# Two edge sums of a graph network: the last chunk of every ring turn comes row by row from SyncE

## The chip, the cores and the metric

The program runs on one core of a Trainium2 chip. The metric is the device time of one execution in microseconds; before the change its median over three runs is 3943.59 us (3941.09 to 3946.39).

## The reference, cut to what matters

```python
# x: 6250 nodes x 256, src/dst/edge_weight: 100000 edges
x = x + gnn0(layernorm(x))      # h = x @ W; agg[row] += edge_weight * h[col]; batch norm; relu
x = x + ffn0(layernorm(x))      # top-k tokens through a gelu MLP
x = x + gnn1(layernorm(x))      # aggr[row] += edge_weight * x[col]; two-layer MLP; row norm
x = x + moe(layernorm(x))       # 8 experts, top 2
```

Both graph layers hold the same sum over edges: for each edge, one row of 1 KB (256 float32) is read by its column number, weighted, and added to the node of its row number. These two sums are what the change touches.

## The kernel before, in words

The kernel first sorts the edges by tile of 128 nodes (the first block, up to about 377 us in the trace), and packs them into 784 chunks (`CHUNKS`) of 128 edges. A chunk that straddles two node tiles is used twice, so there are 832 slots (`SLOTS`), worked off in 52 steps of 16 (`STEPS`, `GB`), four at a time (`GSEM`).

`aggregate` is one such sum and is called twice: with `table[0]` (the first sum, about 385 to 1375 us) and with `through_mlp` set (the second sum, about 1786 to 2798 us). In it:

- GpSimd (POOL) issues one indirect DMA for each chunk (L1081). It brings the chunk's 128 rows of 1 KB from the table in HBM into one of `RING` = 56 places of the tile `got`. Before every pair of chunks it waits on `pairs_summed`, the count of pairs of slots that TensorE has finished, so that a place is free again.
- TensorE (PE) waits for the landing of four chunks at a time (`gathered`), reads the four places of its slots from `slot_ring` into registers (L1167), and multiplies each chunk with a 128x128 routing matrix (L1174). A slot is one product, recorded as two matmuls.
- VectorE (DVE) builds the routing matrices (L1090) and adds each product to the accumulator A of its node tile (L1107).
- Beside it, each finished node tile goes through a small chain on TensorE, ScalarE (ACT) and VectorE: one product and statistics in the first sum (`NodeRows`), a two-layer MLP, two norms and router scores in the second (`GraphTiles`).
- SyncE (SP) is nearly idle. In the first sum it loads and keeps some parameters (until L1060) and then waits. In the second sum it stores each normalised tile to `expert_table`: `store_normal` (L960) waits for the tile, issues one DMA of 128 KB, waits until it has landed (L963) and only then counts `stored` up, on which `normalise` of the next tile waits. There is one buffer `normal`. To find the tile's number SP reads two registers per step from SBUF (L1039, L1041).

The order of the slots and their places in the ring are worked out by VectorE at the end of the first block, in `order_slots` (L515 to L520), and turned by TensorE and stored from there; the block ends when those tables are back in SBUF and the last scatter of edge records has landed.

Of the kernel before, what the change touches and what calls it, by code (L numbers as in the profile page):

```python
# [5 lines left out]
ALU = mybir.AluOpType  # L6
# [8 lines left out]
P = 128  # L15
# [25 lines left out]
RING = 56  # L41
SLOT_COLUMNS = -(-SLOTS // P)
# [13 lines left out]
assert EP * EJ == E and NG * GC == EJ and RUNS_D * RUN * P < BIG and CHUNKS % GSEM == 0 and SLOTS % GB == 0 and RING % GSEM == 0 and NT % GROUP == 0 and GROUPS % 2 == 1  # L56
# [6 lines left out]
class Steps:  # L63
# [28 lines left out]
def build(nc, x, src, dst, edge_weight, g0_w, g0_bias, g0_gamma, g0_beta, f0_wr_in, f0_br, f0_w1, f0_b1_in, f0_w2, f0_b2_in,  # L92
# [14 lines left out]
    with ctx:  # L107
# [103 lines left out]
        with ExitStack() as scope, nc.Block() as block:  # L211
# [164 lines left out]
            def _(dve):  # L376
# [114 lines left out]
                def order_slots():  # L491
# [12 lines left out]
                    for f in range(3):  # L504
# [11 lines left out]
                    s(dve.tensor_tensor(past_ring, chunk_of_slot[:].unsqueeze(2).to_broadcast([P, SLOT_COLUMNS, rings]),  # L516
                                        ring_start[:].unsqueeze(1).to_broadcast([P, SLOT_COLUMNS, rings]), ALU.is_ge))
# [314 lines left out]
        class GraphTiles:  # L832
# [5 lines left out]
            def __init__(self, here):  # L838
                self.tile = FinishedTile(here, "g1_")
                self.wr = here("wr", [P, KD, NE])  # L840
                self.normal, self.normal_t = here("normal", [P, D]), here("normal_t", [P, D])
# [4 lines left out]
                self.normal_ready, self.landed, self.stored = sem("g1_normal"), sem("g1_normal_landed"), sem("g1_normal_stored")  # L846
# [100 lines left out]
            def normalise(self, dve, k, t):  # L947
# [5 lines left out]
                wait(dve, self.stored, k)  # L953
                wait(dve, self.normal_turned, k)
                dve.tensor_scalar(self.normal[:], row(X, t), self.ln_moments[:, 0:1], self.ln_inverse[:, 0:1],
                                  ALU.subtract, ALU.mult).then_inc(self.normal_ready, 1)

            def store_normal(self, sp, k, t):
                sp.wait_ge(self.normal_ready, k + 1)
                sp.dma_start(expert_table[:, 0:D].rearrange("(t p) d -> p t d", p=P)[:, bass.ds(t, 1), :],  # L960
                             self.normal[:].rearrange("p (a d) -> p a d", a=1)).then_inc(self.landed, 16)
                sp.wait_ge(self.landed, 16 * k + 16)
                sp.sem_inc(self.stored, 1)  # L963

            def turn_normal(self, pe, k):
                pe.wait_ge(self.normal_ready, k + 1)
                wait(pe, self.normal_out, k)
                for i in range(KD):
                    ins = pe.transpose(psum[:, self.BANK_OF, i * P:(i + 1) * P], self.normal[:, i * P:(i + 1) * P], ident[:])
# [32 lines left out]

        def aggregate(rows, name, through_mlp, source, local, weight):
# [5 lines left out]
            FINISHES = STEPS - 1  # L1009
            with ExitStack() as scope, nc.Block() as block:  # L1010
                here = lambda what, shape, dt=F32: sb(name + what, shape, dt, scope)
                got = here("got", [P, RING, D])
# [14 lines left out]
                def gathered_after(q):  # L1027

                    earlier = -(-(CHUNKS // GSEM - q % 8) // 8) if through_mlp else 0
                    return (earlier + q // 8 + 1) * (16 * GSEM)  # L1030
# [18 lines left out]
                def _(sp):  # L1049
# [3 lines left out]
                    if not through_mlp:  # L1053
# [6 lines left out]
                        sp.dma_start(f0_first[:].rearrange("p (k n) -> p k n", k=KD), f0_w1.rearrange("(k p) n -> p k n", p=P)).then_inc(params, 16)  # L1060
                        sp.wait_ge(params, 144)
                    if through_mlp:
                        for k in range(FINISHES):
# [1134 lines left out]
```

## Time and profile before

| | |
|---|---|
| median of 3 runs | 3943.59 us (3941.09 to 3946.39) |
| span of the profiled execution | 3521.7 us |
| time of the profiled execution beside its span | not stated; median less span is 421.9 us |
| POOL, indirect DMAs of both sums (L1081) | 1568 x 952 ns |
| first sum, 405 to 1385 us: PE / DVE / ACT / POOL busy | 618 / 611 / 61 / 731 us of 980 |
| second sum, 1787 to 2770 us: PE / DVE / ACT / POOL busy | 702 / 725 / 135 / 745 us of 983 |

The span runs from the first to the last instruction that the profiler recorded. A group's line gives busy time and mean duration, then the idle time of the engine in front of it and what ended that idle time. "issue" is time in which the engine waited for nothing that the profile shows. SPq, ACTq, DVEq and POOLq are the sequencers of the engines: register work and the issuing of DMAs, which don't count as busy.

### The profile page before, as it was taken

How to read it: one execution, taken by the hardware profiler on the slowest of the kernel's cores; microseconds unless marked ns; L12 is line 12 of the kernel's file. 1: busy time of each engine (PE TensorE's matmuls, PEld its weight loads, DVE VectorE, ACT ScalarE, POOL GpSimd, SP SyncE). 2: the span in 40 equal slices, each digit the busy share in tenths (PEclk: the TensorE clock that was granted, in tenths of full speed). 3: DMA queues.
4: the chain of work that ended last, by engine and by line, in shares of the span. 5: the costliest groups of instructions: out<-in, count | busy, mean ns of one | idle time of the engine just before them, and what ended most of it. 6: DMA issues, size and time to landing. Idle time of an engine off the chain costs nothing. (4 is left out here: it accounts for less than half of the span.)

```text
span 3521.7 us, 55765 instructions
## 1 busy us (share of the span) xinstructions
PE 2647.4 (75%) x15311; PEld 2239.6 (64%) x15311; DVE 2613.3 (74%) x6603; ACT 1008.4 (29%) x2073; POOL 2208.3 (63%) x2147
## 2 busy tenths in 40 slices
PE   6888466666666665899967677777776569999998
PEld 4777344454444444789945555555555459999997
DVE  6999566666666666969967777777777778888886
ACT  0011000000000002545511111111111168888886
POOL 0455577777777774345557777777777326666664
PEclk9999687878878787899978888888788779999999
DMA  3011433333333332000133333333333447776775
GB/s 98 10 44 33 120 105 105 105 105 105 105 105 105 105 105 73 1 2 31 37 103 111 113 112 111 113 113 111 113 111 113 133 134 216 213 218 211 219 211 140
DMA packets 164679, 389.01 MB, mean 110 GB/s; under 512 B 46378, under 2 KB 95602, under 8 KB 151019
## 3 DMA queue, kind: packets, MB, share of 16 engines
q0 software_dynamic: 99072, 233.49, 24.4%
q1 hardware_dynamic: 65387, 152.94, 12.8%
q8 instruction: 96, 1.57, 0.2%
q14 instruction: 124, 1.02, 0.1%
HBM read 343.97 MB, written 42.98 MB: 110 GB/s over the span
## 5 line engine op out<-in xcount | busy, mean ns | idle before, releaser
L1081 POOL DMA_INDIRECT g_got<-table,e_source x1568 | 1492.1, 952 | 506.5 <-issue 458.9
L1174 PE MATMUL psum<-g_got,g_route 128*128 x3328 | 1087.2, 485 | 642.0 <-DMA g_got<-table,e_source 253.6
L1174 PEld LDWEIGHTS psum<-g_got,g_route 128*128 128x128 f32 x3328 | 760.9, 239 | 888.4 <-issue 763.5
L1107 DVE TENSOR_TENSOR A<-A,psum 128x256 f32 x1664 | 698.5, 420 | 523.6 <-PE psum L1174 345.1
L1090 DVE TENSOR_SCALAR g_route<-columns,e_local,e_weight 128x128 f32<-128x128 f32 x1664 | 472.5, 363 | 17.7 <-issue 12.9
L368 POOL DMA_INDIRECT records<-rec,place x120 | 148.7, 1239 | 220.6 <-ACT rec L580 122.0
L1582 POOL TENSOR_TENSOR f_ht_lo<-f_ht,f_ht_hi 128x512 fp32r<-128x512 f32 x100 | 133.7, 1341 | 187.8 <-ACT f_ht_hi L1531 182.1
L142 PE MATMUL psum<-e_xt_hi,e_w_hi 128*128 128x256 f32 x832 | 238.0, 286 | 5.5 <-issue 5.3
L142 PE MATMUL psum<-e_w_hi,e_ht_hi 128*128 128x256 f32 x832 | 233.1, 280 | 3.1 <-DVE e_w_lo L1981 3.1
L144 PE MATMUL psum<-e_xt_hi,e_w_lo 128*128 128x256 f32 x832 | 233.8, 281 | 0.0
L143 PE MATMUL psum<-e_xt_lo,e_w_hi 128*128 128x256 f32 x832 | 233.7, 281 | 0.0
L143 PE MATMUL psum<-e_w_lo,e_ht_hi 128*128 128x256 f32 x832 | 233.0, 280 | 0.0
L144 PE MATMUL psum<-e_w_hi,e_ht_lo 128*128 128x256 f32 x832 | 232.8, 280 | 0.0
L1860 POOL DMA_INDIRECT out<-e_y,e_homes x104 | 179.1, 1722 | 63.4 <-POOL e_homes L1856 47.6
L661 PE MATMUL psum<-to_row,value 125*48 125x128 f32 x1600 | 191.1, 281 | 31.5 <-DVE to_row L554 30.8
L661 PEld LDWEIGHTS psum<-to_row,value 125*48 125x48 f32 x1600 | 180.5, 127 | 52.0 <-issue 38.1
L2126 ACT ACTIVATE e_ht<-psum,e_b 128x256 f32<-128x256 f32 x416 | 181.8, 473 | 100.0 <-PE psum L144 100.0
L830 ACT COPY A<-psum 128x256 f32 x52 | 19.4, 372 | 575.3 <-DVE node_stats L818 575.3
L1987 DVE TENSOR_TENSOR e_ht_lo<-e_ht,e_ht_hi 128x512 fp32r<-128x512 f32 x208 | 138.6, 689 | 50.9 <-ACT e_ht_hi L2130 49.4
L1973 DVE TENSOR_TENSOR e_w_lo<-e_w,e_w_hi 128x2048 fp32r<-128x2048 f32 x52 | 119.2, 2293 | 58.4 <-ACT e_w_hi L2135 58.4
L142 PEld LDWEIGHTS psum<-e_xt_hi,e_w_hi 128*128 128x128 f32 x832 | 157.6, 189 | 5.9 <-issue 5.9
L142 PEld LDWEIGHTS psum<-e_w_hi,e_ht_hi 128*128 128x128 f32 x832 | 158.9, 191 | 3.3 <-issue 3.3
(420 smaller groups left out, 5198.5 us busy)
## 6 DMA issues: line engine op xcount, KB each, us to landing
e_w<-in_m_w SPq DMA_DIRECT2D x104, 1024.0 KB, 5.0
g_got<-table,e_source POOLq DMA_INDIRECT x1568, 2.8
expert_table<-g_normal SPq DMA_DIRECT2D x52, 128.0 KB
table<-xn SPq DMA_DIRECT2D x49, 128.0 KB, 1.7
X<-in_x SPq DMA_DIRECT2D x1, 6144.0 KB
table<-f_ring SPq DMA_DIRECT2D x24, 256.0 KB, 2.1
out<-X SPq DMA_DIRECT2D x1, 6144.0 KB
f_w<-in_f_w SPq DMA_DIRECT2D x2, 1024.0 KB, 7.3
```

The lines of the kernel that those rows point to most:

```text
L142: pe.matmul(to, a_hi, b_hi, start=first, stop=False)
L143: pe.matmul(to, a_hi, b_lo, start=False, stop=False)
L144: return pe.matmul(to, a_lo, b_hi, start=False, stop=last)
L368: pool.indirect_dma_start(by_row, bass.IndirectOffsetOnAxis(ap=place[:, g, d:d + 1].bitcast(U32), axis=0), rec[:, g % 2, d, :, :].rearrang ...
L661: ins = pe.matmul(sums_of(u), value[0:EP, u, j, :, :].rearrange("p f c -> p (f c)"), to_row[0:EP, u, j, :], start=j == 0, stop=j == GC - 1)
L1081: pool.indirect_dma_start(got[:, c % RING, :], None, rows, bass.IndirectOffsetOnAxis(ap=source[:, c:c + 1].bitcast(U32), axis=0)).then_inc ...
L1090: ins = dve.tensor_scalar(route[:, (n * GB + j) % (GB + GSEM), :], columns[:], local[:, n * GB + j:n * GB + j + 1], weight[:, n * GB + j:n ...
L1107: dve.tensor_tensor(to, to, sums_of(c), ALU.add).then_inc(added, 1)
L1174: ins = pe.matmul(sums_of(c), route[:, c % (GB + GSEM), :], row(got, at[j % GSEM]), start=True, stop=True)
L1860: pool.indirect_dma_start(out, bass.IndirectOffsetOnAxis(ap=homes[:, u, j:j + 1].bitcast(U32), axis=0), y[:, u, j, :], None, bounds_check= ...
L1987: dve.tensor_tensor(ht_lo[:, u, of], ht[:, of], ht_hi[:, u, of], ALU.subtract).then_inc(h_split, 1)
L2126: act.activation(ht[:, b * MT:(b + 1) * MT], psum[:, 1 + b % 4, 0:MT], ACT.Gelu, bias=b1[:, one, b]).then_inc(hid_out, 1)
```

## The change

In every turn of the ring but the first, the last chunk (numbers 111, 167, ..., 783: 13 chunks of each sum) isn't brought by POOL's indirect DMA. SyncE brings its 128 rows one by one: it loads the row numbers of half a chunk (64 words) from HBM into one partition, reads eight of them into registers with one statement, and issues eight DMAs of one row (1 KB) each with the register as source address (`HandRows.fetch`). These chunks rotate over three places at the end of `got` (`HAND_PLACES`), which grows from 56 to 58 places, so that SyncE may begin up to three turns ahead; it waits on `pairs_summed` for a place. TensorE waits for such a chunk on a semaphore of its own place.

`order_slots` works out the new places with six more VectorE operations. In the second sum, SyncE no longer stores the normalised tiles: ScalarE issues these stores, from two alternating buffers with a semaphore each, and waits for the last two at the end. `normalise` then waits for the store and the transpose of the tile before the last one.

```diff
+HAND = RING - 1
+HAND_PLACES = 3
+PLACES = HAND + HAND_PLACES
+ROUND = HAND_PLACES * RING
...
+def place_of(c):
+    return HAND + c // RING % HAND_PLACES if c % RING == HAND else c % RING
...
-                    rings = CHUNKS // RING
-                    past_ring = passed_of[:, :, 0:rings]
-                    s(dve.tensor_scalar(ring_start[:], columns[:, 1:1 + rings], float(RING), None, ALU.mult))
-                    s(dve.tensor_tensor(past_ring, chunk_of_slot[:]..., ring_start[:]..., ALU.is_ge))
-                    s(dve.tensor_reduce(ring_no, past_ring, AX.X, ALU.add))
+                    def count_started(to, every):
+                        n = (CHUNKS - 1) // every
+                        ...   # the same three operations, n columns wide
+                    count_started(turn_no, RING)
+                    count_started(hand_no, ROUND)
                     s(dve.tensor_scalar(slot_tile_f, slot_values[:, 1, :], rank_tile_f[:, 0:1], None, ALU.add))
-                    dve.scalar_tensor_tensor(ring_no, ring_no, -float(RING), chunk_of_slot[:], ALU.mult, ALU.add).then_inc(map_ready, 1)
+                    s(dve.scalar_tensor_tensor(hand_no, hand_no, -float(HAND_PLACES), turn_no, ALU.mult, ALU.add))
+                    s(dve.scalar_tensor_tensor(ring_no, turn_no, -float(RING), chunk_of_slot[:], ALU.mult, ALU.add))
+                    s(dve.scalar_tensor_tensor(hand_no, ring_no, float(HAND), hand_no, ALU.is_equal, ALU.mult))
+                    dve.tensor_tensor(ring_no, ring_no, hand_no, ALU.add).then_inc(map_ready, 1)
...
-                wait(dve, self.stored, k)
-                wait(dve, self.normal_turned, k)
+                wait(dve, self.stored[k % 2], 16 * (k // 2))
+                wait(dve, self.normal_turned, k - 1)
...
-            def store_normal(self, sp, k, t):
-                sp.wait_ge(self.normal_ready, k + 1)
-                sp.dma_start(expert_table[...], self.normal[:]...).then_inc(self.landed, 16)
-                sp.wait_ge(self.landed, 16 * k + 16)
-                sp.sem_inc(self.stored, 1)
+            def store_normal(self, act, k, t):
+                act.wait_ge(self.normal_ready, k + 1)
+                act.dma_start(expert_table[...], self.normal[:, k % 2:k % 2 + 1, :]).then_inc(self.stored[k % 2], 16)
...
+        class HandRows:
+            LOAD = 8
+            HALF = P // 2
...
+            def ask(self, sp, i, h):
+                c = self.chunks[i]
+                sp.dma_start(self.numbers[:, h, :], kept_fields[0][h * self.HALF:(h + 1) * self.HALF, c:c + 1].rearrange("p a -> a p"),
+                             allow_slow_non_contiguous=True).then_inc(hand_numbers_in, 16)
+
+            def fetch(self, sp, got, rows, pairs_summed, start, end):
+                for r in range(start, min(end, P * len(self.chunks)), self.LOAD):
+                    i, p = divmod(r, P)
+                    h, c = p // self.HALF, self.chunks[i]
+                    if r == 0:
+                        self.ask(sp, 0, 0)
+                    if p == 0 and c >= ROUND:
+                        sp.wait_ge(pairs_summed, (c - ROUND + NT - 1) // 2 + 1)
+                    if p % self.HALF == 0:
+                        sp.wait_ge(hand_numbers_in, 16 * (2 * (self.before + i) + h + 1))
+                    _, nodes = nc.values_load_multi_w_load_instructions(self.numbers[0:1, h, p % self.HALF:p % self.HALF + self.LOAD], ...)
+                    for j in range(self.LOAD):
+                        sp.dma_start(got[p + j:p + j + 1, place_of(c), :], rows[bass.ds(nodes[j], 1), :]).then_inc(hand_landed[(self.before + i) % HAND_PLACES], 16)
+                    if p % self.HALF == 0 and i + h < len(self.chunks):
+                        self.ask(sp, i + h, 1 - h)
...
                             for c in range(first, first + GSEM // 2):
+                                if c in hand.chunks:
+                                    continue
                                 pool.indirect_dma_start(
-                                    got[:, c % RING, :], None, rows,
+                                    got[:, place_of(c), :], None, rows,
...
                             if n >= 3:
                                 tiles_of.keep_normal_turned(act, n - 3)
+                                tiles_of.store_normal(act, n - 3, tile_to_finish(n - 2, mybir.EngineType.Activation))
...
                         tiles_of.keep_result(act, FINISHES)
+                        tiles_of.store_normal(act, FINISHES - 1, tile_to_finish(FINISHES, mybir.EngineType.Activation))
                         tiles_of.keep_normal_turned(act, FINISHES - 1)
```

SyncE's part of both sums is now `hand.fetch(sp, got, rows, pairs_summed, 0, P * CHUNKS)`: in the first sum behind its parameter loads, in the second behind the loads of `GraphTiles`.

## Rows read from the trace of the kernel before

**Rows 1.** The core's span and clock, and POOL's gathers on the page.
```profile
core 0: 3521.7 us, clock 0.868
...
L1081 POOL DMA_INDIRECT g_got<-table,e_source x1568 | 1492.1, 952 | 506.5 <-issue 458.9
```

**Rows 2.** Busy time by stretch: us, PE, PEld, DVE, ACT, POOL, PEclk, DMA share, GB/s.
```profile
405.00:1385.00 980.00, 618.41 (x2163) 468.75 (x2162) 611.05 (x1756) 61.06 (x157) 730.53 (x769) 0.80 0.36 105
1787.00:2770.00 983.00, 701.73 (x2741) 537.79 (x2742) 725.49 (x2286) 134.92 (x447) 744.70 (x783) 0.83 0.39 112
```

**Rows 3.** Timeline of POOL: first and last gather of the first sum, both of the second.
```profile
385.31 0.97 POOL L1081 DMA_INDIRECT g_got<-table,e_source  x1 [9.32 <-DVE e_source L753]
...
1368.60 0.95 POOL L1081 DMA_INDIRECT g_got<-table,e_source  x1 [0.30 <-issue]
...
1786.23 1.02 POOL L1081 DMA_INDIRECT g_got<-table,e_source  x1 [19.94 <-POOLq L1261]
...
2770.30 0.95 POOL L1081 DMA_INDIRECT g_got<-table,e_source  x1 [0.30 <-issue]
```

**Rows 4.** Waits: PE in either sum, POOL in the second (total, times, longest us).
```profile
PE psum L1174 <- DMA g_got<-table,e_source: 143.5, 56, 5.8
...
PE psum L1174 <- DMA g_got<-table,e_source: 110.1, 59, 16.1
...
POOL g_got L1081 <- PE psum L1174: 10.4, 34, 0.3
```

**Rows 5.** Landing of the gathers, 1787 to 2760 us.
```profile
DMA to landing us min/median/max: 2.6/2.8/3.9
```

**Rows 6.** Timeline of SyncE's issued DMAs: start us, us, line.
```profile
362.75 0.25 SPq L335 DMA_DIRECT2D tile_of_rank_row<-rank_tile_i  x1
...
365.16 0.76 SPq L340 DMA_DIRECT2D step_rank<-slot_map  x1
...
367.00 0.36 SPq L342 DMA_DIRECT2D tile_of_rank<-tile_of_rank_row  x1
...
403.21 0.43 SPq L1058 DMA_DIRECT2D f_br_row<-in_f_br  x1
...
404.19 0.29 SPq L1059 DMA_DIRECT2D f_b<-in_f_b_in  x1
404.53 0.38 SPq L1060 DMA_DIRECT2D f_w<-in_f_w  x1
...
1786.94 0.29 SPq L865 DMA_DIRECT2D g_b<-in_g_b  x1
...
1788.48 0.47 SPq L868 DMA_DIRECT2D router_bias<-in_m_br  x1
```

**Rows 7.** SyncE's store of a normalised tile, by instruction (ns min/median/max).
```profile
L960 SPq FUSED_REGOPS  x52: 37/37/42, 1866.5 to 2795.2; - x52
L960 SPq MOVE expert_table<-g_normal x52: 29/29/43, 1866.6 to 2795.3; - x52
L960 SPq DMA_DIRECT2D expert_table<-g_normal x52: 332/332/366, 1866.7 to 2795.3; - x52
```

**Rows 8.** Register loads: one value on SP, one and four values on DVE.
```profile
L1041 SPq TENSOR_LOAD <-tile_of_rank x51: 267/273/292, 1789.6 to 2785.5; - x51
...
L1039 DVEq TENSOR_LOAD <-finish_tile x102: 305/318/333, 440.8 to 2782.8; - x102
...
L1096 DVEq TENSOR_LOAD <-slot_tile x416: 337/344/611, 414.3 to 2773.7; - x139
```

**Rows 9.** Timeline of DVE in `order_slots`.
```profile
358.54 0.26 DVE L516 TENSOR_TENSOR over<-chunk_of_slot,ring_start 128x98 f32<-128x98 f32 x1
...
359.39 0.17 DVE L520 SCALAR_TENSOR_TENSOR slot_columns<-slot_columns,chunk_of_slot 128x7 f32<-128x7 f32 x1
```

**Rows 10.** Timeline of ACT at the end of the second sum.
```profile
2791.87 0.27 ACT L988 ACTIVATE row_numbers<-psum,g_ln_scale 128x8 f32 x1 [1.28 <-PE psum L981]
2792.04 0.19 ACT L903 ACTIVATE g_root<-g_root 128x1 f32<-128x1 f32 x1
```

More of the change, by code:

```diff
@@ L1001, in build, with __init__, wait_landed @@
         gathered = [sem(f"gathered{u}") for u in range(8)]
+        class HandRows:
+            LOAD = 8
+            HALF = P // 2
+            def __init__(self, turns, before):
+                self.chunks = [RING * k + HAND for k in turns]
+                self.before = before
+                self.numbers = expert[:].rearrange("a (h p) -> a h p", h=2)
+            def ask(self, sp, i, h):
[12 more added lines that the diff above has]
+                        sp.wait_ge(hand_numbers_in, 16 * (2 * (self.before + i) + h + 1))
+                    _, nodes = nc.values_load_multi_w_load_instructions(
+                        self.numbers[0:1, h, p % self.HALF:p % self.HALF + self.LOAD], engines=(mybir.EngineType.SP,), min_val=0, max_val=NT * P - 1,
+                        skip_runtime_bounds_check_because="a source is a node")
+                    for j in range(self.LOAD):
+                        sp.dma_start(got[p + j:p + j + 1, place_of(c), :], rows[bass.ds(nodes[j], 1), :]).then_inc(hand_landed[(self.before + i) % HAND_PLACES], 16)
+                    if p % self.HALF == 0 and i + h < len(self.chunks):
+                        self.ask(sp, i + h, 1 - h)
+            def wait_landed(self, pe, q):
+                for i, c in enumerate(self.chunks):
+                    if c // GSEM == q:
+                        pe.wait_ge(hand_landed[(self.before + i) % HAND_PLACES], 16 * P * ((self.before + i) // HAND_PLACES + 1))
@@ L1003, in aggregate, with gathers_of @@
+        hand_numbers_in, hand_landed = sem("hand_numbers_in"), [sem(f"hand_landed{u}") for u in range(HAND_PLACES)]
+        turns = range(1, CHUNKS // RING)
+        hands = (HandRows(turns, 0), HandRows(turns, len(turns)))
+        def gathers_of(q, hand):
+            return [c for c in range(q * GSEM, (q + 1) * GSEM) if c not in hand.chunks]
         def aggregate(rows, name, through_mlp, source, local, weight):
@@ L1009, in aggregate @@
             FINISHES = STEPS - 1
+            hand = hands[through_mlp]
             with ExitStack() as scope, nc.Block() as block:
                 here = lambda what, shape, dt=F32: sb(name + what, shape, dt, scope)
-                got = here("got", [P, RING, D])
+                got = here("got", [P, PLACES, D])
                 route = here("route", [P, GB + GSEM, P])
@@ L1027, in gathered_after @@
                 def gathered_after(q):
-                    earlier = -(-(CHUNKS // GSEM - q % 8) // 8) if through_mlp else 0
-                    return (earlier + q // 8 + 1) * (16 * GSEM)
+                    own = sum(len(gathers_of(at, hand)) for at in range(q % 8, q + 1, 8))
+                    before = sum(len(gathers_of(at, hands[0])) for at in range(q % 8, CHUNKS // GSEM, 8)) if through_mlp else 0
+                    return 16 * (before + own)
                 def sums_of(c):
@@ L1060, in _ @@
                         sp.dma_start(f0_first[:].rearrange("p (k n) -> p k n", k=KD), f0_w1.rearrange("(k p) n -> p k n", p=P)).then_inc(params, 16)
+                        hand.fetch(sp, got, rows, pairs_summed, 0, P * CHUNKS)
                         sp.wait_ge(params, 144)
                     if through_mlp:
-                        for k in range(FINISHES):
-                            tiles_of.store_normal(sp, k, tile_to_finish(k + 1, mybir.EngineType.SP))
-                        tiles_of.store_normal(sp, FINISHES, last_tile(sp))
+                        hand.fetch(sp, got, rows, pairs_summed, 0, P * CHUNKS)
                 @block.gpsimd
@@ L1790, in build @@
             added = [sem("e_added0"), sem("e_added1")]
-            finished = sem("e_finished")
             QUARTER = HB * MT // 4
```

31 lines of the change are left out of this document (21 added, 10 removed).

## The prediction

> **What bounds the kernel now.** I read the span first, then the page's costliest groups, the busy time by stretch, POOL's timeline, the waits, and last SyncE's issued DMAs. The span is 3521.7 us against a median of 3943.6 us; the page gives no time of its own for the profiled execution. I take the 421.9 us between them as lying around the span and unchanged, so that a microsecond saved in the span is one saved in the time [rows 1].
>
> In both sums no engine is full by its busy time: POOL leads with 731 of 980 us and 745 of 983 us, DVE and PE have 611 to 725 [rows 2]. But POOL's gathers are a clock. The first sum's 784 start between 385.31 and 1368.60 us, the second's between 1786.23 and 2770.30 us. That is 983.29 / 783 = 1.2558 us and 984.07 / 783 = 1.2568 us each: 0.95 us of work and 0.30 us of "issue", in which POOL waits for nobody [rows 3]. Its waits for TensorE in the second sum are 34 of at most 0.3 us, as long as that same gap, so they cost nothing; TensorE on its side waits 143.5 us and 110.1 us in all for landings of gathers [rows 4]. So the sums last as long as 784 gathers take, plus the landing of the last one (2.8 us) and the end of the last tiles [rows 5].
>
> **Part 1: 13 gathers fewer per sum.** A hand chunk is skipped in POOL's loop, and nothing takes its place there. 13 x 1.256 = 16.3 us per sum, 32.7 us for both. The last chunk, 783, is a hand chunk itself; it must only be there early enough. For the saving to arrive, TensorE and VectorE must take 56 chunks in 55 x 1.256 = 69.1 us instead of 70.3 us. The landing waits of 143.5 and 110.1 us are the reserve, of which 16.3 us each would be used [rows 4]. This part is all of the gain.
>
> **Part 2: what SyncE needs for it.** A row is a register operation, a move and a DMA, as in the store of a tile by a register: 37 and 29 ns, and the DMA [rows 7]. Between SyncE's instructions lie 0.04 to 0.05 us (404.19 + 0.29 to 404.53) [rows 6]. The trace has the same shape of DMA twice, one row of 1 KB into one partition, issued right behind another DMA: 0.29 us both times (b2, L1059 and L865) [rows 6]. So one row costs 0.037 + 0.029 + 0.29 + 3 x 0.04 = 0.474 us, and 128 rows 60.7 us. Eight numbers are read with one load: on DVE four values cost 344 ns and one 318 ns, so 9 ns for each further one, and on SP 273 + 7 x 9 = 334 ns, with its gap 0.374 us; 16 of them are 6.0 us [rows 8]. The two loads of row numbers gather 64 single words each; the nearest is the one with 52 (0.76 us), so 1.6 us [rows 6]. With 0.1 us for waits a turn costs SyncE **68.4 us**, against the 69.1 us that POOL leaves it.
>
> It need not even be below. In the first sum SyncE is free at 404.9 us [rows 6] and, after the first row numbers (0.8 + 2.8 us), begins its first chunk at 408.5 us; chunk 111 would be due from POOL's beat at 385.3 + 110 x 1.256 = 523.4 us. Less one turn that is 45.9 us ahead (landings on both sides cancel). In the second sum it begins at 1788.95 + 3.6 = 1792.6 us, 62.7 us ahead by the same sum [rows 3, 6]. Over 13 chunks nothing is late as long as a turn stays under 69.1 + 45.9 / 13 = 72.6 us and 73.9 us. The places of the ring allow SyncE to be more than a hundred chunks ahead, so its wait on `pairs_summed` is not what limits it.
>
> The bounds for the row's DMA are 0.25 us (one row stored after a DMA, L335) and 0.36 us (one short row loaded behind two other one-partition loads, L342); the widest row that it could be like is 0.43 us, a DMA over 128 partitions right behind another (L1058) [rows 6]. A turn is then 63.3, 77.4 or 86.3 us. I take 0.29 us, since those two are the same copy. The saving is eaten up where 26 turns are late by 30.2 us in all beyond both reserves of 108.6 us: at 5.3 us per turn over 69.1, so at 0.335 us for the DMA. The margin is 0.05 us per row, which is small. Reading eight numbers in two loads instead of one would cost 5.7 us per turn, and use it up as well.
>
> The Trainium skill speaks against the row here: "DMA: Bandwidth & Descriptors", in the table of instruction costs for descriptors made in hardware under the section on why a DMA increments its semaphore by 16, puts one copy at 512 sequencer cycles for generations before the newest, which at the 1.2 GHz that the page "Trainium Kernel Development and Optimization" (NeuronCore Architecture) states for SyncE is 0.427 us. The trace has both: 0.43 us for 128 partitions in a series, and 0.29 us for one row. By the page's figure the sum would be that of the second rival below.
>
> **Part 3: the stores move to ScalarE.** It issues 52 of them, each a register operation, a move and a DMA of 0.33 us, 0.5 us with gaps, and reads two registers first, 0.7 us with its register operation [rows 7, 8]: 1.2 us per step of 19 us, on an engine that is busy 135 us of 983 [rows 2]. The wait in it, for the normalised tile, stands behind the copy of the same tile's transpose and so is over; what is queued behind it is the next tile's staging copy, and for that TensorE's transpose. In the steady part that is hidden. At the end it isn't: the store of the last tile but one stands before the copy, the scores and the root of the last tile, and the root follows the scores without a gap [rows 10]. I charge **+1.2 us**, between 0 and 3 us (three stores in the tail). SyncE's wait for each landing goes, and with it DVE's for a free buffer; DVE's wait shows nowhere, so I count no gain.
>
> **Part 4: the map.** Three narrow counting operations and three more of 7 columns, 0.17 to 0.26 us with 0.04 us between [rows 9]: 6 x 0.22 = **+1.3 us** in front of the tables that the first block's end waits for. Below, these tables leave later and get out of the way of the last scatters, which could give that back and some more; I keep 0 to +1.3 us, and -4 us for a lucky order.
>
> **Sum.** -32.7 + 1.2 + 1.3 = -30.2 us: 3943.6 - 30.2 = **3913 us**.
>
> **The rivals.**
>
> *SyncE becomes the bound.* If the row's DMA costs 0.36 us instead of 0.29, a turn lasts 77.4 us, 8.3 us more than POOL's. The first sum is then late by 13 x 8.3 - 45.9 = 62 us and the second by 108 - 62.7 = 45 us; less 30.2 us that is +78 us, 4021 us. It decides from 0.335 us on. For it: the row from L342, and that no row of the trace shows many such DMAs in a series, nor eight values read by SP. Against: the two equal copies, both behind another DMA.
>
> *A flat price per DMA.* If each costs 0.43 us whatever its size, a turn is 86.3 us, and the same sum gives 13 x 17.2 x 2 - 108.6 - 30.2 = +308 us, 4252 us. Only this would agree with the page named above; the two rows at 0.29 us and the one at 0.25 us speak against it.
>
> *TensorE and VectorE take over.* If the pair can't go faster than now, the 13 gathers are hidden and only the 2.5 us remain: 3946 us. For it: in the second sum DVE is busy 74% and PE waits often for DVE. Against: 110 us of waits for landings in that sum, 143 us in the first.
>
> *Rows late by a little.* Between 0.32 and 0.335 us for the DMA a part of the gain is lost, 3920 to 3943 us; it is inside the range.
>
> **How the numbers follow.** I give 0.62 to the forecast (its own range 3905 to 3925 us: the low end with the lucky order of part 4, the high end with a turn of about 74 us or twice the tail), 0.08 to rows late by a little, 0.07 to the pair as the bound, 0.18 to SyncE as the bound and 0.05 to the flat price. A measurement here can't tell less than 0.2% (7.9 us) from no change. Faster by more has the forecast and half of the late rows, 0.66. Within 0.2% lie the other half and most of the pair, 0.10. Slower is the rest, 0.24. The range goes from 3905 to 3985 us: it takes in the forecast, the partial cases, the pair, and the lower part of SyncE as the bound, and leaves out about 2 in 10.
>
> **What the profile after would show.** Right: 1542 gathers of 0.95 us with an unchanged beat of 1.256 us; first to last gather of a sum 967 us instead of 983; SyncE's row DMAs at 0.29 us and a turn of 68 us, the last row of a sum issued well before POOL's last gather; no wait of TensorE on row copies. SyncE as the bound: waits of TensorE that end with a row copy, from a chunk in the middle of the sum on and longer each turn, and POOL's waits for TensorE of more than 0.3 us. The pair as the bound: POOL waiting for TensorE in a sum where SyncE is ahead. The prediction would be wrong most easily by the price of one row on SyncE, which is counted 3328 times; after that by a beat of POOL that changes when another queue is busy, and by time around the span that grows with some ten thousand instructions more.

## The result and the profile after

| | median | range | runs |
|---|---|---|---|
| kernel before | 3944.99 us | 3941.09 to 3948.93 | 4 |
| changed kernel | 4795.55 us | 4775.57 to 4819.91 | 4 |

The ratio is 1.2146 [1.2097, 1.2196], so the change costs 850 us, where 30 us of gain were forecast. The profiled execution of the changed kernel took 4819.91 us by its own time. One run of E16 below (4114.41 us, at a granted clock of 0.668 where the others have 0.83) is left out of its median and ratio.

The page of the changed kernel, with the core's span first (busy, mean ns, idle before and what ended most of it):

```profile
core 0: 4818.1 us, clock 0.759
...
L1154 POOL DMA_INDIRECT g_got<-table,e_source x1542 | 1467.2, 952 | 1717.5 <-PE psum L1248 1016.6
L1248 PE MATMUL psum<-g_got,g_route 128*128 x3328 | 1022.2, 468 | 1225.8 <-DMA g_got<-table 1082.3
L1180 DVE TENSOR_TENSOR A<-A,psum 128x256 f32 x1664 | 699.3, 420 | 1791.3 <-PE psum L1248 1040.9
```

The span is within 1.8 us of the execution's own time: nothing lies around it. The 26 gathers fewer are there, each still 952 ns [rows 1]. Against that TensorE now waits 1082.3 us, and the name behind the arrow is `g_got<-table` without `e_source`: the row copies of SyncE. GpSimd and VectorE wait as long for TensorE.

SyncE's row statement in the changed kernel, first in the first sum, then in the second (x count: ns min/median/max, first and last start), with who waited for it:

```profile
L1055 SPq DMA_DIRECT2D g_got<-table x1664: 2/225/1407, 422.6 to 2042.1; - x185
...
  PE psum L1248: 629.1, 13
...
L1055 SPq DMA_DIRECT2D g_got<-table x1664: 3/225/1422, 2465.1 to 4061.7; - x185
...
  PE psum L1248: 453.1, 13
```

All 13 hand chunks of both sums are late, by 48 us and 35 us each on average. A chunk takes SyncE (2042.1 - 422.6) / 13 = 124.6 us and (4061.7 - 2465.1) / 13 = 122.8 us, where the prediction had 68.4 us. The median of the DMA, 225 ns, is even below the 0.29 us that was assumed. The price depends on what GpSimd does. The same statement in two stretches of 20 and 22 us: the first from 424 us on, where GpSimd gathers without a pause up to 437.5 us and then stops; the second in GpSimd's pause from 676 to 719 us, with the load of eight numbers there:

```profile
L1055 SPq FUSED_REGOPS  x5: 700/718/1386, 424.0 to 440.9; - x5
L1055 SPq MOVE g_got<-table x5: 690/700/710, 425.4 to 442.3; - x5
L1055 SPq DMA_DIRECT2D g_got<-table x5: 17/700/726, 426.8 to 443.7; - x5
...
L1055 SPq MOVE g_got<-table x41: 29/29/29, 690.0 to 710.8; - x41
L1055 SPq DMA_DIRECT2D g_got<-table x41: 224/225/260, 690.0 to 710.9; - x41
L1055 SPq FUSED_REGOPS  x41: 37/37/37, 691.1 to 712.0; - x41
...
L1051 SPq TENSOR_LOAD <-expert x6: 777/780/780, 690.3 to 711.2; - x6
```

Five rows in the first stretch, 4.2 us each, and 41 in the second. A register operation of 37 ns takes 718 ns in the first stretch, a move of 29 ns takes 700 ns: it isn't the DMA that is dear, it is every kind of instruction that SyncE uses for a row. The slow pace outlasts the gathers: it ends at 444.5 us, 7 us behind the last one, and over 136 stops of GpSimd 2.3 us behind it in the median. GpSimd's timeline in between shows how the two come to terms:

```profile
657.97 0.95 POOL L1154 DMA_INDIRECT g_got<-table,e_source  x1 [3.92 <-remote]
...
675.47 0.95 POOL L1154 DMA_INDIRECT g_got<-table,e_source  x1 [0.30 <-issue]
719.73 0.94 POOL L1154 DMA_INDIRECT g_got<-table,e_source  x1 [43.31 <-PE psum L1248]
```

TensorE stands before a hand chunk, GpSimd runs out of places and stops for 43 us, and in that stop SyncE goes at full pace and finishes the chunk. Of the 3328 rows 2188 start in stops (more than 1.3 us behind the start of a gather), 1140 beside gathers.

### The profile page after: what moved, and what is told of

It is laid out like the page before. It is cut to its first block and busy times, and to the rows that moved or that the text cites. A ratio compares the mean times of both kernels' runs of the same rounds, so it can differ in the third digit from the quotient of the medians.

```text
span 4818.1 us, 66165 instructions
## 1 busy us (share of the span) xinstructions
PE 2648.9 (55%) x15311; PEld 2255.3 (47%) x15311; DVE 2603.8 (54%) x6609; ACT 1004.1 (21%) x2073; POOL 2180.2 (45%) x2121
## 5 line engine op out<-in xcount | busy, mean ns | idle before, releaser
L1154 POOL DMA_INDIRECT g_got<-table,e_source x1542 | 1467.2, 952 | 1717.5 <-PE psum L1248 1016.6
L1248 PE MATMUL psum<-g_got,g_route 128*128 x3328 | 1022.2, 468 | 1225.8 <-DMA g_got<-table 1082.3
L800 PE MATMUL psum<-ident,g_rows 128*128 128x128 f32 x208 | 57.2, 369 | 412.6 <-ACT A L848 204.2
L800 PEld LDWEIGHTS psum<-ident,g_rows 128*128 128x128 f32 x208 | 31.5, 184 | 450.5 <-ACT A L848 221.5
L912 PE MATMUL psum<-g_w,g_hidden 128*128 128x256 f32 x208 | 83.3, 541 | 187.5 <-ACT g_hidden L906 161.6
```

The source lines that it names most:

```text
L1154: pool.indirect_dma_start(got[:, place_of(c), :], None, rows, bass.IndirectOffsetOnAxis(ap=source[:, c:c + 1].bitcast(U32), axis=0)).then_ ...
L1248: ins = pe.matmul(sums_of(c), route[:, c % (GB + GSEM), :], row(got, at[j % GSEM]), start=True, stop=True)
```

## The experiments

The kernel before ran beside each of them on the same chip. Six chips took part, each on one occasion only: A (E0 to E3), B (E4 to E7), C (E8 to E10), D (E11 to E13), E (E14 to E16) and F (E17). The kernel before took 3928.97, **3530.34**, 3932.16, 3925.18, 3924.41 and 3945.89 us on them. On B its 31 runs lie between 3523.71 and 3537.91 us, on the others no run is below 3915 us. A number below is always against the kernel before of its own chip.

**E0, the kernel before, traced on chip A.** No edit.

> The kernel before, unchanged, profiled and timed once more. Its page had a span of 3521.7 us beside a median of 3944 us; the changed kernel has 4818.1 us beside 4819.9 us. If the 422 us lie around the span (my assumption in the prediction), span and time will differ by some 420 us again. The rival: span and time differ by 2 us as in the changed kernel, and the page of before was an execution of another, faster course; then the first and last gather of a sum lie further apart than 983 us, and TensorE, VectorE or SyncE show the slow pitch that the changed kernel shows (instructions 1.4 us apart while POOL gathers).

3926.79 us, ratio 0.9990 [0.9975, 1.0005], and a span of 3927.0 us. The trace of the kernel before, once more, on this chip: the core, the gathers of either sum, and TensorE's matmuls of either sum.

```profile
core 0: 3927.0 us, clock 0.818
...
L1081 POOL DMA_INDIRECT g_got<-table,e_source x784: 943/949/1041, 387.2 to 1537.1; - x196
...
L1081 POOL DMA_INDIRECT g_got<-table,e_source x784: 943/949/1178, 1978.0 to 3146.6; - x196
...
L1174 PE MATMUL psum<-g_got,g_route x1664: 379/379/791, 403.1 to 1566.1; 128*128 x185
...
L1174 PE MATMUL psum<-g_got,g_route x1664: 376/379/791, 1985.3 to 3172.3; 128*128 x185
```

The 405 us between this span and the 3521.7 us of [rows 1] lie in the sums: their gathers take 1149.9 and 1168.6 us from first to last in place of 983.3 and 984.1 us [rows 3], and TensorE ends 29.0 and 25.7 us behind the last gather in place of 6.1 and 5.0 us. That is 166.6 + 184.5 + 22.9 + 20.7 = 395 of the 405 us. One period of it, on VectorE, GpSimd, ScalarE and TensorE:

```profile
809.86 5.35 PE L1174 MATMUL psum<-g_got,g_route 128*128 x24
...
819.30 0.95 POOL L1081 DMA_INDIRECT g_got<-table,e_source  x1 [0.30 <-issue]
823.12 0.98 DVE L1107 TENSOR_TENSOR A<-A,psum 128x256 f32 x2 [9.31 <-remote]
823.77 0.95 POOL L1081 DMA_INDIRECT g_got<-table,e_source  x1 [3.52 <-remote]
...
827.79 0.45 PE L782 MATMUL psum<-ident,g_rows 128*128 128x128 f32 x1 [12.58 <-ACT A L830]
```

TensorE's 24 matmuls are over at 815.2 us. VectorE, which adds their sums, goes on only at 823.1 us, 3.8 us after GpSimd has begun its last gather; GpSimd itself waits 3.5 us for a count that TensorE had long reached, since TensorE ran nothing between 815.2 and 827.8 us. Single gathers are as quick as ever (0.95 us every 1.25 us). What is late is the news between engines, and it arrives when GpSimd stops. Sixteen gathers and one such stop of 3.5 us make a period of 23.3 us, where sixteen alone took 20.1 us.

**E1, no hand chunk.** All gathers by GpSimd, the new map, the new places and ScalarE's stores kept.

```diff
-        turns = range(1, CHUNKS // RING)
+        turns = range(1, 1)
```

> The changed kernel, but POOL gathers all 784 chunks of each sum and SyncE fetches no row; the three places, the map and ScalarE's stores stay. Theory (the row fetch is all of the loss): 3945 us, +1 to +4 us by the map and the tail, or some us below if the stores' waits mattered. Rival (the stores from ScalarE or the map slow the sums): clearly above 3960 us.

3925.13 us, ratio 0.9995 [0.9977, 1.0013]. Parts 3 and 4 of the change cost nothing that can be measured; an interval of about 7 us to either side can't show the +2.5 us that were forecast for them. The 850 us are in the rows.

**E2, three hand chunks per sum.**

```diff
-        turns = range(1, CHUNKS // RING)
+        turns = (3, 7, 11)
```

> The changed kernel with only turns 3, 7 and 11 fetched row by row, so 3 chunks of each sum instead of 13. SyncE has four turns, over 270 us, for each chunk. Theory A (SyncE's rows come too late at 1.2 to 1.4 us each while POOL gathers, and nothing else is hurt): no wait for rows is left, and the 6 gathers fewer give 7.5 us against the kernel with none: -5 us against before. Theory B (SyncE's row copies slow the gathers, TensorE or VectorE while they run): slower than the kernel without rows, in proportion to the 768 rows: a quarter of the loss of 850 us is +200 us.

3943.80 us, ratio 1.0032 [1.0021, 1.0044]. Neither theory: 15 us slower, where A said 5 us faster and B 200 us slower. SyncE is nearly in time, but not quite. Its 128 rows take 143 to 209 us, and it has not the four turns that the expectation gave it: its place comes free only at 547.7 us, and TensorE stands before the first of these chunks at 736 us. TensorE waits for row copies twice in the first sum (12.5 and 9.2 us) and not at all in the second. The second sum got longer even so: its gathers take 1184.7 us, against 1162.7 us in E1. So lateness alone isn't the loss, and the six gathers saved (7.5 us) are outweighed.

**E3, row copies that nobody waits for.** E1, and SyncE copies 13 x 128 rows per sum from a fixed address to a scratch tile.

```diff
+                        sp.dma_start(scratch[p:p + 1, :], rows[p:p + 1, :]).then_inc(landed, 16)
```

> As the kernel without rows, but SyncE issues 13 x 128 copies of one row in each sum, from a fixed address into a tile that nobody reads, so without register work and without loads of numbers; POOL gathers everything and nobody waits for SyncE except the end of the sum. It measures the price of a row copy while POOL gathers. Theory A1 (each instruction of SyncE takes 1.4 us while POOL gathers): 1.4 us for each copy, 179 us for 128, and the sum ends with SyncE at 2330 us instead of 983. Theory A2 (the copy alone is dear): the same. Theory C (the price was in loads and register work): 0.25 to 0.45 us for each copy, the sums end on time. If POOL is not waited on and its beat stays at 1.256 us, the copies don't slow the gathers; if its beat grows, they do.

3964.42 us, ratio 1.0085 [1.0064, 1.0106]. SyncE's work costs the others 35 us by itself, though nobody waits for it. And the trace shows that the hold-up isn't the same all along a stretch of gathers. GpSimd gathers sixteen times from 827.3 to 847.1 us; these are SyncE's copies in its first 5 us, the next 5 us and the last 10 us:

```profile
L1065 SPq DMA_DIRECT2D g_scratch<-table x15: 23/252/284, 827.3 to 831.6; - x15
...
L1065 SPq DMA_DIRECT2D g_scratch<-table x6: 7/700/727, 832.4 to 836.7; - x6
...
L1065 SPq DMA_DIRECT2D g_scratch<-table x9: 17/704/710, 838.0 to 847.2; - x9
```

Beside the first three gathers of a stretch the copies come every 0.295 us, as in pauses. From the fifth on they come every 0.72 us, and towards the end of the stretch mostly every 1.40 us (medians by place in the stretch, over both sums). So 128 copies take 53 to 87 us, where theory A1 had 179 us.

**E4, increments in place of the copies**, on chip B.

```diff
-                        sp.dma_start(scratch[p:p + 1, :], rows[p:p + 1, :]).then_inc(landed, 16)
+                        sp.sem_inc(landed, 1)
```

> As the kernel with 3328 idle copies, but in place of each copy SyncE only counts a semaphore up that nobody waits for: no DMA at all. With copies one instruction took 0.70 us (median) while POOL gathered without a pause, 0.295 us where it paused. Theory D (SyncE's sequencer, not the DMA, is held to one instruction per 0.7 us while POOL gathers): 0.7 us per increment again in those stretches, far less in the pauses, and 13 x 128 of them in 900 to 1100 us if they were always held. Theory E (the copy itself is held: its descriptors or its completion): the increments take under 0.1 us each everywhere. Time: with copies it was 1.0085 of before; if the loss came from DMA traffic, this is at before's 3929 us; if from SyncE's instructions, between 3929 and 3965 us.

3533.48 us, ratio 1.0007 [0.9997, 1.0018]. On this chip nothing is held up: an increment every 0.06 us, gathers in 983.6 and 983.3 us without a pause. It could tell nothing apart here and was run again as E10. The same holds for E5 to E7: their expectations give times for a chip on which the kernel before takes 3929 us, and they met this one.

**E5, hand chunks that nobody fetches**, from turn 3 on (11 per sum): `fetch` issues nothing and TensorE doesn't wait for them. Chip B.

```diff
-        turns = range(1, CHUNKS // RING)
+        turns = range(3, CHUNKS // RING)
...
-                                hand.wait_landed(pe, q)
```

> Chunks 223, 279, ..., 783 of each sum are fetched by nobody (11 chunks per sum; TensorE multiplies what lies in their place, so the sums are of other data): 22 gathers fewer, no row copies, no wait. It prices part 1 of my sum alone. As the prediction had it, each gather fewer gives 1.256 us: -27.6 us against the kernel without rows (3925 us), 3898 us. The rival, from the profile of before taken again: POOL stands still 167 and 181 us in the sums, waiting, in a rhythm of 16 gathers and a pause, and what sets the sum is how fast the finished pairs come back; then fewer gathers only lengthen the pauses: within 5 us of 3925 us.

3531.97 us, ratio 1.0002 [0.9993, 1.0012]. The gathers take 969.7 and 969.5 us, as short as 11 fewer should make them, and yet the time is that of before. Where it was given back is shown with E7.

**E6, a shorter lead of GpSimd in the kernel before.** Chip B.

```diff
-                            if q >= 8:
-                                done = max(done, first_slot_after(q - 8) // 2 + 1)
+                            if q >= 4:
+                                done = max(done, first_slot_after(q - 4) // 2 + 1)
```

> The kernel before with one number changed: POOL may be 4 groups of chunks ahead of TensorE's finished pairs instead of 8. In the profile of before taken again, POOL gathers 16 chunks without a pause, TensorE's finished pairs reach VectorE and POOL only when POOL has stopped (VectorE idles 9.3 us in each step, POOL 3.5 us). Theory F (what TensorE has finished is held up while POOL gathers without a pause, and is let through in a pause): shorter bursts, about 8 gathers, with a pause each; VectorE's and POOL's idle stretches get shorter and more frequent. If a pause costs its 3.5 us each time, the sums get longer by 49 x 3.5 = 170 us each (slower, 4250 us); if the pause shrinks with the burst, no change; if the hold-up only begins after a burst of more than 8 gathers, the sums fall towards 984 us, and the time to 3600 us. Rival G (the rhythm comes from TensorE or VectorE being too slow): waiting longer for them makes no burst shorter than the work allows, 3929 us or a little more.

3529.36 us, ratio 0.9997 [0.9987, 1.0007]: nothing, where nothing is held up. See E15.

**E7, all 13 hand chunks from fixed addresses.** The changed kernel without loads of numbers and register work; TensorE waits for the rows. Chip B.

```diff
-                        sp.dma_start(got[p + j:p + j + 1, place_of(c), :], rows[bass.ds(nodes[j], 1), :]).then_inc(...)
+                        sp.dma_start(got[p + j:p + j + 1, place_of(c), :], rows[p + j:p + j + 1, :]).then_inc(...)
```

> The changed kernel with the 13 chunks still fetched row by row and waited for, but each row from a fixed address (other rows than the reference's): the register operation, the move and the loads of eight numbers are gone, so a row is one instruction instead of three and an eighth. Theory D (price per instruction of SyncE, 0.7 us while POOL gathers): a turn of SyncE takes 80 to 90 us as in the kernel with idle copies, against 82 us of a turn of the sum: rows hardly late, 3950 to 4050 us instead of 4796. Theory H (what counts is 3328 copies that somebody waits for, whatever they take on SyncE): still above 4500 us.

3528.54 us, ratio 0.9992 [0.9982, 1.0003]. The rows come every 0.295 us. Here are the gathers of the second sum and the gathers of the experts' blocks, of E6 (the work of before) and then of E7:

```profile
L1081 POOL DMA_INDIRECT g_got<-table,e_source x784: 942/946/1204, 1788.9 to 2772.7; - x196
...
L1873 POOL DMA_INDIRECT e_rows<-expert_table,e_nodes x104: 948/1150/1818, 2861.0 to 3475.0; - x104
```

```profile
L1151 POOL DMA_INDIRECT g_got<-table,e_source x771: 942/949/1204, 1772.8 to 2743.3; - x193
...
L1948 POOL DMA_INDIRECT e_rows<-expert_table,e_nodes x108: 952/1022/1812, 2831.8 to 3474.9; - x108
```

The experts' stage begins 29.2 us sooner with 13 gathers fewer per sum, and lasts four gathers longer: 108 in place of 104, two for a block of tokens. The wrong rows send other tokens to the experts, and two blocks more are needed (E5 has 108 as well); with (3474.9 - 2831.8) / 53 = 12.1 us for a block they cost 24 us. So E5 and E7 don't show that the saving is lost. Without those blocks E7 would stand at about 3504 us, 26 us below before. That is an estimate, and for rows of one instruction.

**E8, the changed kernel again**, on chip C, and E11 and E14, the same on D and E.

> The changed kernel once more, nothing edited, to learn how it stands where the kernel before shows 3530 us and where it shows 3930 to 3945 us. Theory K (the place decides): the +850 us belong to executions in which GpSimd's gathers hold up the others (before at 3930 to 3945 us, pauses of GpSimd, each instruction of SyncE 0.70 us long while gathers run). There: 4780 to 4820 us again, SyncE's turn 114 to 127 us. If instead the kernel before shows about 3530 us here, a row should cost SyncE 0.41 us as in the pauses of the trace of after, so 128 rows with 16 loads take 60 to 69 us, which is at or under the 69 us of 55 gathers, and the kernel should show about 3500 us (two sums of 983.5 us less 13 x 1.256 = 16.3 us, less what the last chunk's lateness costs), 3500 to 3530 us. Rival (the edit alone decides): over 4000 us wherever it runs.

4748.15 us, ratio 1.2048 [1.2016, 1.2080]. E11: 4737.29 us, 1.2054 [1.2025, 1.2083]. E14: 4743.33 us, 1.2073 [1.2028, 1.2118]. E8 came 32 us below what it expected (4780 to 4820 us), E11 and E14 within (4730 and 4720 to 4820 us). None of the three met a chip like B, so how the changed kernel does there stays open.

**E9, E3 again**, on chip C beside E10.

> The kernel in which GpSimd gathers all rows and SyncE beside it issues 2 x 13 x 128 copies of one row that nobody waits for (leaves nothing of the computation out). Where the kernel before shows 3930 to 3945 us: +25 to +40 us and a pitch of 0.70 us per copy while gathers run, as seen. Where it shows 3530 us: copies every 0.30 us throughout (as the fixed rows showed), no pause of GpSimd, time within 0.3% of before.

3970.15 us, ratio 1.0089 [1.0068, 1.0109], as on chip A.

**E10, E4 again**, on chip C.

> The same with an increment of a semaphore in place of each copy. It tells what is dear on SyncE while GpSimd gathers, if this is where gathers hold the others up. Theory D (the DMA issue is held up): increments every 0.06 us as in the quick executions, time as before. Theory E (each instruction of SyncE that touches a semaphore or a queue is held up): increments every 0.5 to 0.7 us too, time +10 to +40 us. Where the kernel before shows 3530 us: 0.06 us again and nothing told apart.

3943.33 us, ratio 1.0028 [1.0012, 1.0044]. The increments between 412.2 and 424 us, in E10 and, for the same stretch, in E4 on chip B:

```profile
L1064 SPq EVENT_SEMAPHORE  x9: 699/700/710, 412.3 to 423.5; - x9
```

```profile
L1064 SPq EVENT_SEMAPHORE  x196: 17/17/17, 412.2 to 424.0; - x196
```

The same program, the same stretch: 9 increments of 0.70 us, 1.40 us apart, against 196 of 17 ns. Theory D of this expectation, that the DMA alone is held up, is refuted (in E4's expectation the two letters are the other way round); theory E stands, and more widely than it was put, since in the changed kernel moves and register operations are held up too.

**E12, E7 again**, on chip D.

> The changed kernel with its rows from fixed addresses: no loads of numbers and no register work, one instruction per row in place of three; it brings other data than the sum needs, so its output and the number of experts' blocks differ (two blocks of about 12 us more, as its trace on another chip had). Where before shows over 3900 us: theory E (every instruction of SyncE held up for 0.70 us while gathers run) says 0.70 us per row, a turn of 75 to 90 us against 69 us, so rows late by a little each turn and 4000 to 4150 us, far below 4750. Rival (the wait for the rows itself costs, whatever their price): over 4500 us. Where before shows 3530 us: as before, 0.46 us per row.

3956.01 us, ratio 1.0074 [1.0046, 1.0101]. Mine was 4000 to 4150 us, too high: I had left out that the gathers themselves take longer here. A turn of 55 gathers lasts about 82 us with GpSimd's stops, and 128 rows of one instruction took 55 to 89 us, so they were in time: the trace shows no wait of TensorE that ends with a row copy. The rival is refuted with it. E12 has the two blocks more as well (about 24 us), so the rest of it stands about 7 us above before.

The fair comparison for its 26 gathers fewer is E9, which issues as many copies of one instruction beside all 784 gathers. The experts' gathers in E12 and then in E9:

```profile
L1948 POOL DMA_INDIRECT e_rows<-expert_table,e_nodes x108: 948/996/1814, 3261.8 to 3900.5; - x108
...
L1963 POOL DMA_INDIRECT e_rows<-expert_table,e_nodes x104: 949/1026/1811, 3300.0 to 3914.3; - x104
```

The experts' stage begins 38.2 us sooner in E12 (E9 is of chip C; E3, of chip A, has 3302.4 us). The 26 gathers were worth 32.7 us in the forecast. So they gain about what they should here too, and SyncE's 3328 instructions, which cost 35 to 38 us by themselves (E3, E9), take it back: in E0, without either, that stage begins at 3259.2 us.

**E13, E2 again**, on chip D.

> The changed kernel with three chunks of each sum by SyncE (turns 3, 7 and 11), nothing left out. Six gathers of 1.256 us less = 7.5 us less work of GpSimd. Where before shows 3530 us: 3520 to 3526 us (ratio 0.997 to 0.999). Where it shows over 3900 us: +0.1 to +0.5%, as the first time, since held-up instructions of SyncE outweigh the gathers.

3948.48 us, ratio 1.0050 [1.0033, 1.0067]. Slower again, by as much as was expected. TensorE waits once in each sum for a row copy, 14.2 and 17.3 us.

**E15 and E16, the kernel before with a shorter lead**, on chip E: 16 chunks (the edit of E6) and 8 chunks (`q - 2`) in place of 32.

> The kernel before with GpSimd held 16 chunks ahead of the sums in place of 32; nothing left out. Theory L (long uninterrupted stretches of gathers hold the updates up): where before shows 3920 to 3945 us GpSimd would wait sooner and the updates come sooner, 3750 to 3900 us. Rival M (the rhythm is set by the ring of 56 places, which already holds GpSimd closer than the lead does): within 0.3% of before, as it was where before showed 3530 us.

> The same with 8 chunks of lead in place of 32. Theory L: where before shows 3920 to 3945 us, stretches of at most 8 gathers, updates sooner, 3600 to 3850 us. Rival M2 (a short lead only adds waits: every 8 gathers GpSimd waits for TensorE, whose updates come late): 4000 to 4300 us. Where before shows 3530 us: 0 to +3%, since the landing of a chunk (2.6 us) and the check of the lead stand in the way each time.

E15: 3891.28 us, ratio 0.9897 [0.9864, 0.9930]. E16: 3906.56 us, 0.9940 [0.9915, 0.9965]. Both beat both kernels, by 1.0% and 0.6%, less than theory L said, and not by its way. E15's gathers and matmuls in the first sum:

```profile
L1081 POOL DMA_INDIRECT g_got<-table,e_source x784: 940/947/1053, 388.4 to 1532.3; - x196
...
L1174 PE MATMUL psum<-g_got,g_route x1664: 376/379/792, 405.9 to 1547.8; 128*128 x185
```

The gathers take 1143.9 us, only 6 us less than in E0, and still in stretches of sixteen with stops of 3.5 us; in the second sum they take 1177.6 us, 9 us more than in E0. What is shorter is TensorE's backlog behind the last gather: 15.5 us in place of 29.0 us, and in the second sum 15.4 in place of 25.7 us. These 23.8 us are most of the 27.5 us between the two spans (E0 is of chip A; the kernel before was not traced on E). E16's backlog is shorter still, 5.4 and 6.9 us, but its gathers take 1164.1 and 1190.6 us, so a lead of 8 chunks wins less than one of 16. On chip B, where the backlog is 6 us, the same edit gave nothing (E6).

**E17, the changed kernel with a lead of 16 chunks**, on chip F.

> The changed kernel with GpSimd held 16 chunks ahead in place of 32, nothing left out. Where before shows about 3530 us: 3495 to 3530 us by theory K, over 3700 us by the rival that the edit is bad everywhere. Where before shows 3920 to 3945 us: the gathers are not fewer and SyncE's three instructions per row stay at 0.70 us beside them, so the turn stays 112 to 127 us and the time 4650 to 4800 us; the gain of the lead (TensorE's lag behind the last gather, 13 us per sum in the kernel before) is 30 us at most here, since TensorE waits for SyncE's rows. Rival: GpSimd, stopped sooner, leaves SyncE quieter stretches, turn under 105 us, under 4550 us.

4774.99 us, ratio 1.2093 [1.2072, 1.2115]. The shorter lead does nothing for the rows; a turn stays near 118 us.

## Why the prediction was wrong

**The step that failed first is the one about the span:** "I take the 421.9 us between them as lying around the span and unchanged". No execution traced since has more than 2 us around its span. Nearly all of those 422 us stand for another regime of the same kernel, in which the timed runs were and the traced one was not. The trace that the prediction read was like chip B's (3530 us); the runs by which the change was judged were like those of the other five. E0 shows the difference: single instructions of GpSimd as before, but updates and SyncE's instructions held up while it gathers.

**The step that cost the 850 us is the price of a row**, "0.474 us, and 128 rows 60.7 us". A turn can now be put together from what the trace after shows. Of its 128 rows 1140 / 26 = 44 start beside gathers, in the 69.1 us that 55 gathers last. The other 84 come at 0.408 us with a load of 0.81 us for each eight, 34.3 + 8.5 = 42.8 us. That makes 112 us. GpSimd stops about five times in a turn (141 stops in all), and the hold-up outlasts each stretch of gathers by some 2.3 us, which adds up to 12 us. The estimate is then 112 to 124 us; the trace has 114 to 128 us for all but the first and the last chunk of each sum. This is an account of the parts, and a rough one. From first to last gather the sums became 1986.9 - 387.5 = 1599.4 us and 4013.2 - 2459.0 = 1554.2 us, against 1149.9 and 1168.6 us in E0: +835 us. TensorE's longer end behind the last gather, 60.2 and 53.5 us in place of 29.0 and 25.7 us, is +59 us. Together that is 894 us, against 891 us between the two spans. E12 is the test of it: with one instruction per row in place of three and an eighth, and all else as in the changed kernel but the rows' contents, the loss is 31 us, where the changed kernel loses 812 us on the same chip (E11).

**The same price on a quiet SyncE was nearly right, by two errors that cancel.** The row is 0.408 us, not 0.474 us, since its DMA takes 0.225 us. The load of eight values takes 780 ns, where 334 ns had been drawn on from VectorE's loads [rows 8]. A turn is 128 x 0.408 + 16 x 0.81 = 65.2 us and two loads of numbers of 0.5 us each, an estimate of 66 us in place of 68.4 us. That the two came out alike was luck.

The Trainium skill puts a copy at 512 cycles on generations before the newest ("DMA: Bandwidth & Descriptors", under "Why a DMA increments its semaphore by 16 and not by 1"), which the prediction turned into an estimate of 0.427 us. The 225 ns of a row's DMA contradict it for this shape, and it says nothing of the 0.70 us beside gathers.

**The beat of GpSimd** held as the price of a gather. Where nothing is held up, 11 or 13 gathers fewer shortened each sum by 13 to 14 us (E5, E7). Where GpSimd's stops set the rhythm, 26 fewer were worth about their 32.7 us as well (E12 against E9). What the sum put at nothing is what SyncE's own instructions do to the others: 35 to 38 us for 3328 of them (E3, E9). So on these chips the change would have gained about nothing even with rows in time. Gathers left out with no SyncE instruction in their place were not run on such a chip.

**Parts 3 and 4** (+1.2 and +1.3 us) were small enough: E1 shows no change within about 0.2%.

**The rival that came true is "SyncE becomes the bound"**, with the sign that was named for it (waits of TensorE that end with a row copy) but from the first hand chunk on, and by a turn of 123 us in place of 77 us. Its price was bounded by rows of quiet moments, all between 0.25 and 0.43 us [rows 6]; no row of the old trace shows a SyncE instruction beside gathers as these chips run them. The 422 us between the page's span and the median were the one sign.

**Open:** why nothing was held up on chip B and much on the other five (each was used on one occasion, so the runs don't tell the chip from the occasion), what it is in GpSimd's indirect DMAs that does it, and what the changed kernel takes on a chip like B. That the hold-up begins some gathers into a stretch and outlasts it speaks for work that is piled up by the gathers, not for the instruction that GpSimd is in, but no run tests this.

## What to carry to other kernels

Before a profile is used, hold its span against the timed runs; if the two differ by more than the executions' own spread, the profile shows another regime, and its slack and its beat are not those of the runs. An idle engine is cheap help only as long as its instructions run at their own length beside what the busy ones do: measure one row's worth of it in place before counting it 3328 times, count instructions, not only DMAs, and count what they cost the others. A change that takes work from one engine should be tried first with the work left undone and nothing in its place, but with the data kept, as data can change how much work follows.

## What the runs showed of the hardware

- While GpSimd issues indirect DMAs one behind the other (0.95 us each, every 1.25 us), SyncE's instructions are held up on five of six chips: a semaphore increment of 17 ns, a move of 29 ns, a register operation of 37 ns and a one-row DMA of 225 ns all take 0.70 us, 0.70 to 1.40 us apart (E10, trace after).
- The hold-up grows along a stretch of gathers: none beside the first three, 0.72 us per copy from the fifth on, mostly 1.40 us at the end (E3), and it outlasts the last gather by 2.3 us in the median (trace after).
- Updates of TensorE reach VectorE late in the same way, when GpSimd stops: 7.9 us behind the last matmul in the period shown, where VectorE stood idle for 9.3 us (E0). The sixth chip shows nothing of all this, and the kernel before is 10% faster there (3530 against 3924 to 3946 us).
- SyncE's own work slows the rest in turn on such chips: 3328 copies that nobody waits for cost 0.9%, 3328 increments 0.3% (E9, E10). On chip B 3328 increments cost nothing (E4).
- A load of eight registers takes 780 ns on SyncE (trace after), more than double the 344 ns of four on VectorE [rows 8].
- On a quiet SyncE the DMA instruction of a one-row copy takes 0.225 us with a register address, with a row every 0.408 us (trace after); with a fixed address 0.252 us, with a row every 0.295 us (E7).
